# Recurrent layer with gated branch on one core: exponentials and logs of the next batch's z in four successive slots, third tile in another PSUM bank

## What is computed

```python
xn = _layernorm(x)                                   # (4, 512, 512)
u, gate = split(xn @ W_in.T)                         # 1024 + 1024 channels
u = silu(causal_conv4(u) + conv_b)
dt, Bm, Cm = split(u @ Wx.T)                         # 32 + 16 + 16, each RMS-normed
delta = softplus(dt @ Wdt.T + dt_bias)               # z = dt @ Wdt.T + dt_bias
def step(state, xs):                                 # scan over the 512 rows
    dA = exp(d_t[..., None] * A)
    state = dA * state + (d_t * u_t)[..., None] * B_t[:, None, :]
    y_t = einsum('bdn,bn->bd', state, C_t)
y = (ys + u * D_param) * silu(gate)
s = y @ W_out.T
g = silu((silu(xn @ w_gate.T) * (xn @ w_up.T)) @ w_down.T)
out = x + s * g
```

## Time and profile before

| | |
|---|---|
| median of 3 runs | 1135.0 us (1133.61 to 1135.99) |
| profiled execution, its own time | 1132.72 us |
| its span, first to last instruction | 1130.9 us |
| busy: PE, DVE, POOL, ACT | 93%, 92%, 85%, 62% of the span |
| last chain, by engine | PE 49%, DVE 26%, POOL 9%, issue 9%, ACT 6% |
| scan pairs of slots 58, in three batches, start at | 306.34, 570.04, 833.75 us |

### The profile page before, as it was taken

One profiled execution on the slowest core, in us unless ns is written; L12 is line 12 of the kernel. 1 busy time (PEld: TensorE's weight loads), 2 busy tenths in 40 slices (PEclk: granted clock), 3 DMA queues, 4 the chain that ended last, 5 costly groups with the idle time before them and its releaser, 6 DMA issues.

```text
span 1130.9 us, 14921 instructions
## 1 busy us (share of the span) xinstructions
PE 1051.1 (93%) x5072; PEld 751.4 (66%) x5072; DVE 1045.5 (92%) x1255; ACT 703.9 (62%) x1155; POOL 958.6 (85%) x524
## 2 busy tenths in 40 slices
PE   5989987989999999989999999998999999999767
PEld 4767765667567785666758786665858787555444
DVE  4599999999999999999999999999999999988895
ACT  5668657775665875576575877476665666355440
POOL 3578998999988899699978899789989899878871
PEclk9989998999999999999999999999999999999988
DMA  4647662633334454343325554243324442334410
GB/s 143 227 155 251 203 222 87 223 121 103 105 112 167 178 187 149 103 158 116 119 72 180 176 184 162 94 159 132 111 81 161 143 163 90 131 122 168 125 61 37
DMA packets 46550, 160.66 MB, mean 142 GB/s; under 512 B 5355, under 2 KB 5611, under 8 KB 37004
## 3 DMA queue, kind: packets, MB, share of 16 engines
q1 hardware_dynamic: 46332, 159.66, 41.1%
q10 hardware_dynamic: 144, 0.07, 0.0%
HBM read 135.33 MB, written 24.38 MB: 141 GB/s over the span
## 4 chain that ended last, share of the span: by engine, by line
PE 49%; DVE 26%; issue 9%; POOL 9%; ACT 6%; DMA 0%; DVEq 0%; SPq 0%; POOLq 0%
PE pj L1209 15%; DVE sb_h L1148 14%; PE hT L1501 10%; PE pj L1410 7%; DVE sb_yT L1066 6%; PE pj L1444 5%; POOL sb_dBu L882 4%; PE pj L1475 3%; PE pj L1227 2%; DVE sb_un L958 2%; PE pj L1519 2%; ACT dA L650 2%; POOL sb_yT L840 2%; PE pj L1214 1%; DVE sb_S L1092 1%
## 5 line engine op out<-in xcount | busy, mean ns | idle before, releaser
L882 POOL TENSOR_TENSOR sb_dBu<-sb_v,sb_bb 128x1024 f32<-128x1024 f32 x254 | 602.5, 2383 | 56.6 <-DVE sb_h L1148 41.9
L1148 DVE TENSOR_TENSOR_SCAN sb_h<-dA,sb_dBu 128x512 f32<-128x512 f32 x512 | 596.7, 1207 | 18.4 <-ACT dA L650 10.3
L650 ACT ACTIVATE dA<-sb_delta,sb_apar 128x512 f32<-128x512 f32 x510 | 346.9, 689 | 262.2 <-DVE sb_h L1148 259.6
L1209 PE MATMUL pj<-sb_x_hi,sb_w_sp 128*128 128x512 f32 x1208 | 341.2, 405 | 15.7 <-DVE sb_un L958 12.7
L1501 PE MATMUL hT<-sb_ident,sb_h 128*128 128x128 f32 x2048 | 284.9, 281 | 46.9 <-DVE sb_yT L1066 36.1
L1501 PEld LDWEIGHTS hT<-sb_ident,sb_h 128*128 128x128 f32 x2048 | 241.6, 144 | 129.6 <-issue 48.1
L1209 PEld LDWEIGHTS pj<-sb_x_hi,sb_w_sp 128*128 128x128 f32 x1208 | 218.0, 190 | 77.2 <-issue 23.5
L1066 DVE SCALAR_TENSOR_TENSOR sb_yT<-hT,sb_cs,sb_yT 128x512 f32<-128x512 f32 x342 | 242.5, 735 | 24.1 <-PE hT L1501 23.0
L840 POOL TENSOR_TENSOR sb_yT<-sb_yT,sb_part 128x512 f32<-128x512 f32 x134 | 172.0, 1283 | 46.0 <-ACT sb_part L753 46.0
L1209 PE MATMUL pj<-sb_x_lo,sb_w_sp 128*128 128x512 f32 x604 | 164.2, 394 | 0.0
L753 ACT ACTIVATE sb_part<-hT,sb_cs_act 128x512 f32<-128x512 f32 x134 | 91.5, 683 | 91.0 <-PE hT L1501 85.2
(11 more groups left out here) (143 smaller groups left out, 783.9 us busy)
## 6 DMA issues: line engine op xcount, KB each, us to landing
sb_w_sp<-w_cache SPq DMA_DIRECT2D x55, 1024.0 KB, 4.8
sb_ring<-w_ring SPq DMA_DIRECT2D x67, 512.0 KB, 3.7
sb_bb<-b_rows SPq DMA_DIRECT2D x128, 256.0 KB, 3.7
w_cache<-sb_w_sp SPq DMA_DIRECT2D x19, 1024.0 KB, 4.9
sb_xio<-x SPq DMA_DIRECT2D x7, 1024.0 KB, 7.1
out<-sb_xio SPq DMA_DIRECT2D x3, 1024.0 KB, 5.7
sb_xio<-x SPq DMA_DIRECT2D x4, 256.0 KB, 3.5
out<-sb_xio SPq DMA_DIRECT2D x4, 256.0 KB, 2.0
```

The lines of the kernel that those rows point to most:

```text
L650: nc.scalar.activation(dA[g % 2][:, :], delta[:, j, :], ACT.Exp, scale=apar[:, j, n:n + 1]).then_inc(dA_done, 1)
L882: nc.gpsimd.tensor_tensor(dBu[:, dbu_buffer(s), :, :], v[:, j:j + 2, :], bb[:, i % B_RING, :].unsqueeze(1).to_broadcast([P, 2, T]), ALU.mu ...
L1148: nc.vector.tensor_tensor_scan(h[:, i % 2, 2 * part + e, :], dA[g % 2][:, :], dBu[:, dbu_buffer(s), e, :], 0.0, ALU.mult, ALU.add).then_in ...
L1209: done = nc.tensor.matmul(bank[:, :], w[:, kk * P:(kk + 1) * P], xs[:, kk, :], start=(p == 0), stop=(p == len(products) - 1))
```

## The change

It acts at the ends of batches 0, 1 and 2. ACT's exp and log of the four z tiles move from slots 57, 58, 60, 61 to 58, 59, 60, 61; DVE's L1134 from slots 58, 59, 61, 62 to 59, 60, 61, 62. The table load stays in slot 57. PE makes z in the same slots as before, 54, 55, 57, 58, but tile 2 goes to bank pj0 and tile 3 to pj3. For this the waits change: tile 2 waits for the silu that reads pj0 (g_done), tile 3 for the first zd_done, `ffn` q = 0 (bank pj0) for the third zd_done where it waited for a silu, q = 2 (bank pj2) for the second zd_done where it waited for the fourth. The bank pj3's next user, in slot 1', waits for the fourth zd_done where it waited for the third. POOL's and SP's lists are as they were.

```diff
-Z0_AT, Z0_BANK = (54, 55, 57, 58), (3, 2, 3, 2)
+Z0_AT, Z0_BANK, Z0_LOG = (54, 55, 57, 58), (3, 2, 0, 3), 58
...
-                    if s == Z0_AT[0] + 3:
+                    if s == Z0_LOG - 1:
...
                         nc.scalar.preload_act_table_set("natural_log_exp_and_others")
-                    if s - 3 in Z0_AT:
-                        j = Z0_AT.index(s - 3)
+                    j = s - Z0_LOG
+                    if 0 <= j < JH:
                         softplus_direct(b + 1, j, pj[Z0_BANK[j]])
...
-                    if s - 4 in Z0_AT:
-                        j = Z0_AT.index(s - 4)
+                    j = s - Z0_LOG - 1
+                    if 0 <= j < JH:
                         dve.wait_ge(sp_done, (b + 1) * KD + j + 1)
...
-                            pe.wait_ge(zd_done, (b - 1) * JH + 3)
+                            pe.wait_ge(zd_done, b * JH)
...
-                        elif j > 1:
-                            pe.wait_ge(zd_done, b * JH + j - 1)
+                        elif j == 2:
+                            pe.wait_ge(g_done, b * KH + 3)
+                        elif j == 3:
+                            pe.wait_ge(zd_done, b * JH + 1)
                         to_delta(b + 1, j, pj[Z0_BANK[j]])
...
-                    elif q < 2:
-                        pe.wait_ge(g_done, (c - 1) * KH + 3 + q)
+                    elif q == 0:
+                        pe.wait_ge(zd_done, c * JH - 1)
+                    elif q == 1:
+                        pe.wait_ge(g_done, c * KH)
                     elif q == 2:
-                        pe.wait_ge(zd_done, c * JH)
+                        pe.wait_ge(zd_done, c * JH - 2)
```

## The result

The changed kernel takes 1140.01 us, median of 16 runs (1137.97 to 1142.0), against 1135.1 us (1133.03 to 1139.11, 16 runs) for the kernel before: ratio 1.004, 95% interval 1.003 to 1.0051. It is slower by 4.9 us where 4.6 were forecast.

A forecast was written before the change was run, and what follows sets the result against it. With PE, DVE and POOL nearly full, PE was read to cover DVE's stall, and POOL's late dBu to delay the chain: 3 x 1.53 = 4.6 us on the median 1135.0 gives 1139.6 us, range 1136.3 to 1141.8.

The forecast's parts named there:

- the stall at slot 58: DVE's scans wait 1.31 us for ACT's decays; the change cuts this to 0.15, worth 0 because PE covers it.
- The margin of 0.05 us at slot 60: DVE's addition of slot 60 starts at 316.22, just behind PE's transposes, which end at 316.17.
- The wait for PE that the removed stall was to turn into: Before DVE's addition of slot 60: the time DVE gains becomes waiting for PE, up to 0.9 us.
- The two waits of DVE: DVE's scans of slots 62 and 1' wait for POOL's late dBu: 0.73 us, then 0.8 us more, 1.53 in all.
- The sum: Over the three batch ends: 3 x 1.53 = 4.6 us slower.
- POOL's pace: POOL's run without a pause beside the moved L1134: taken as unchanged, price between 0 and 0.68 us.
- PE's new waits: `ffn` q = 0 starts 0.1 to 0.2 us later, covered by PE's idle 0.55 us ahead of 328.73.
- Rival 1: PE's rows between 304 and 319 hide slack, so the stall is worth its time: +2.0 us, about 1137, chance 0.13.
- 2: Rival: POOL's L822 doesn't hold dBu back, so the kernel is faster: -2.6 us, 1132.4, chance 0.07.
- rival 3: No change, 1135: PE bounds throughout and DVE's slack behind slot 62 hides the late dBu; chance 0.12.
- rival 4: POOL contention or PE's new wait as well, 0.68 us a batch on top: +6.6 us, 1141.6, chance 0.05.

The follow-up runs named there:

- e1: The changed kernel with POOL's first L822 moved from slot 61 to slot 62, behind dBu of 62 and an addition: 1134.49 us, 0.9997 of the kernel before.
- e2: The changed kernel with tile 1's L1134 back in slot 59, behind the first L1134: 1134.44 us, 0.9992 of the kernel before.
- e8: The kernel before with ACT's first exp made three times ahead of slot 58's decays: 1136.97 us, 1.0023 of the kernel before.
- e4: The changed kernel's banks and PE waits, with all ACT and DVE slots as in the kernel before: 1134.87 us, 1.0002 of the kernel before.
- e3: The changed kernel with ACT's old slots and L1134 in 58, 60, 61, 62, so only tile 1's is later than before: 1140.82 us, 1.005 of the kernel before.

## Why the prediction was right

- **What bounds, and the stall at slot 58.** It was read as covered by PE: right. The change took 1.14 us from it in every batch, and with POOL out of the way none of that reaches the next batch (growth in e1 and e2: 0.08 and 0.00 us). The margin of 0.05 us at slot 60 was read rightly, but behind it there is some cover left: in e8, 0.73 of the further 1.26 us come through, against 0.7 to 0.9 expected, and the rest goes where DVE waited 0.18 us for ACT before slot 61's scans and then for PE's transposes at 319.61; e8 has neither wait.
- **DVE.** Tile 1's L1134 was put 3.46 us later; it starts at 319.46, less 2.59 is 316.87, 3.49 later. The wait for PE that the removed stall was to turn into was put at up to 0.9 us before slot 60; it is 0.73 there. Another 0.53 us come before the addition of slot 58, which I hadn't seen: PE's tiles for it are there at 308.02, and DVE, which got to it at 308.59 before, is now 1.14 us earlier.
- **POOL.** L822 was put at 317.59 and starts at 320.21 - 2.59 = 317.62. Its wait was put near 5.3 us and is 5.65, since with ACT's earlier L753 POOL also got to it 0.3 us earlier. The two waits of DVE were put at 0.73 and 0.80 us and are 0.66 and 0.69. To each belong 0.09 us more, by which neighbours on DVE overlap where nothing is waited for: 0.75 + 0.78 = 1.53 us, behind the 0.07 by which the L1134 in slot 60 had made DVE's own list late at slot 62.
- **The sum.** 1.53 us a batch predicted, 1.60 measured, 4.6 and 4.8 in all; the medians differ by 4.9. DVE's own lateness does not explain the 0.07 that are missing, since it ends in the wait for POOL at slot 1'; POOL's side does. Less the 2.59, its pair of dBu for slots 1' and 2' starts at 334.38 - 2.59 = 331.79, just as forecast (329.37 + 3.46 - 1.03 = 331.80). The dBu of slot 1' then takes 2.42 us in the chain where the prediction used 2.37, and the scans start 0.03 us behind its end, a step from POOL to DVE that the sum left out.
- **POOL's pace.** It was taken as unchanged, with a price of 0 to 0.68 us a batch left open for the moved L1134; 0 was the right end, but not for a reason that the prediction gave. L822 waits for the moved L1134, so that one is over at 319.46 + 0.68 = 320.14, before POOL's run starts at 320.21, and can't slow it. What the trace does show is the third L1134, at 323.60, now beside the dBu of slot 62: this dBu took 2.39 us, against 2.36 with none beside it. The rule of the Trainium skill (GPSIMD Engine Reference, Specifications), that instructions of VectorE contend with GpSimd where they have two inputs in SBUF, makes it 0 for L1134, and the trace agrees to within this 0.03 us.
- **PE's new waits.** 0.1 to 0.2 us was said, covered. In the trace `ffn` q = 0 starts at 324.42, less 2.59 is 321.83, 0.34 late, and PE's idle 0.55 us at slot 62 is still 0.56, though there PE waits for a DVE that is itself late. e4, where DVE is not, shows the price: 0, with 0.38 us of the 0.55 left.
- **The rivals.** Rival 1 (PE's rows hide slack) and 2 fall with e1 and e2, rival 3 with the result, rival 4 with POOL's pace and e4.

Where a page's advice would have led: the Trainium skill (Perfetto Trace Analysis, Optimization Strategy) has one look for the gaps on the most contended engine and start what they wait for sooner. Read for DVE, 92% busy beside PE's 93%, the most visible gap is the 1.31 us at slot 58. Here it was closed and the time didn't move (e1, e2), because without it DVE only waits for PE, whose tiles come no earlier.

## What to carry to other kernels

Removing a wait on a busy engine gains something only if the next engine that it meets isn't later anyway: follow it to that meeting and compare the two arrival times (here 316.22 and 316.17) before paying for its removal. When an instruction is moved, look who waits for it, and then at what stands behind the waiter in its fixed list. For each instruction there, the loss is the delay less the pauses on the way and less its own margin, and the largest of these losses counts (here 3.46 - 2.73 = 0.73 at slot 62, 3.46 - 1.03 - 0.90 = 1.53 at slot 1'). And a repeated pattern makes 1.6 us readable in a trace whose whole length scatters by several.

## What the runs showed of the hardware

The scatter between executions has a face in these traces. At its first products, where both kernels are the same, PE did two groups of four matmuls of 128x512 in 1.09 us each in the trace of before, and in 1.91 and 1.71 us in that of the change, so that PE is 1.4 us later behind them, of the 2.4 us by which slot 0 is late. Timeline of PE, the change:

```profile
17.29 1.91 PE L1197 MATMUL hT<-sb_x_hi,sb_w_sp 128*128 128x512 f32 x4
19.00 1.71 PE L1200 MATMUL hT<-sb_x_lo,sb_w_sp 128*128 128x512 f32 x4
```

The rows of stretches show a granted clock of 1.00 there in both traces. In e3's trace the same two groups took 1.91 and 1.83 us, and there the row shows 0.52, near the lower of the two levels (columns: stretch, its length, busy time and count of PE, PE's weight loads, DVE, ACT and POOL, then clock, DMA share and GB/s):

```profile
17.00:20.00 3.00, 3.00 (x9) 2.37 (x8) 0.18 (x1) 0.00 (x0) 1.01 (x1) 0.52 0.69 221
```

So the lower clock is the likely cause in the change's trace too, with the clock not rightly recorded; that is not shown.

In the last batch both kernels have PE waiting 0.50 and then 1.79 us for DVE, close together, and then eight matmuls of the down product. Before they took 3.60 us at a granted clock of 1.00; after, 5.00 us, with the granted clock at 0.50 (1.2 of 2.4 GHz) for the first 2 us. Timeline of PE in the change, then the row of a stretch:

```profile
1002.61 0.66 PE L1507 MATMUL hT<-sb_ident,sb_h 128*128 128x128 f32 x4 [1.79 <-DVE sb_yT L1057]
1003.20 0.98 PE L1326 MATMUL pj<-sb_ident,sb_gT 128*128 128x128 f32 x4
1003.98 5.00 PE L1481 MATMUL pj<-sb_ring,sb_S 128*128 128x512 f32 x8
...
1003.90:1005.90 2.00, 2.00 (x5) 0.97 (x4) 2.00 (x3) 1.17 (x2) 0.81 (x2) 0.50 0.00 0
```

The same pauses stand in both programs, so they alone don't decide the clock, and the lower clock is not the change's doing: the kernel with only the banks changed (e4), equal to before in every slot up to there within 0.4 us, has them too and took 5.30 us for the same eight. Timeline of PE before, then in e4:

```profile
996.30 3.60 PE L1475 MATMUL pj<-sb_ring,sb_S 128*128 128x512 f32 x8
...
996.60 5.30 PE L1480 MATMUL pj<-sb_ring,sb_S 128*128 128x512 f32 x8
```

What decides between the two levels there stays open. That is 1.4 to 1.7 us of the scatter at one place. In all, 2.6 us ahead of slot 58 and 1.9 in the last batch are why the profiled executions differ by 9.3 us and the medians by 4.9.
